# Making the ternary ffn weights inside the context attention instead of beside the projection and the ffn

## The reference

```
x = x + cross_attention(layernorm(x), ctx_2048)      # self attention and context attention, then projection
x = x + sparse_attention(layernorm(x))               # pairwise scores, top 6 keys
def absmean_quant(w):                                # w1: 2048 x 512, w2: 512 x 2048
    scale = mean(abs(w)); return sign(w) * (abs(w) >= 0.7 * scale)
h   = gelu(einsum('bsd,fd->bsf', layernorm(x), absmean_quant(w1)) + b1)
out = x + einsum('bsf,df->bsd', h, absmean_quant(w2)) + b2
```

## Time and profile before

| | |
|---|---|
| median of 3 runs | 2142.95 us (2142.57 to 2144.84) |
| the profiled execution, its own time | 2141.61 us |
| its span, first to last instruction | 2140.3 us |
| busy: PE, DVE, ACT, POOL | 91%, 55%, 44%, 31% |
| moved by DMA | 255.73 MB |
| mean granted TensorE clock | 0.961 |

### The profile page before, as it was taken

One profiled execution on the slowest core, in us unless ns is written; L12 is line 12 of the kernel. 1 busy time (PEld: TensorE's weight loads), 2 busy tenths in 40 slices (PEclk: granted clock), 3 DMA queues, 4 the chain that ended last, 5 costly groups with the idle time before them and its releaser, 6 DMA issues. The chain is left out here.

```text
span 2140.3 us, 30622 instructions
## 1 busy us (share of the span) xinstructions
...
## 2 busy tenths in 40 slices
...
GB/s 197 188 239 178 109 158 118 146 90 130 130 149 84 144 120 111 100 160 134 105 116 122 137 107 135 132 124 84 144 121 115 74 41 274 142 21 3 1 79 20
DMA packets 213130, 255.73 MB, mean 119 GB/s; under 512 B 62120, under 2 KB 132392, under 8 KB 212464
## 3 DMA queue, kind: packets, MB, share of 16 engines
...
q10 hardware_dynamic: 8448, 0.43, 0.2%
q0 software_dynamic: 2048, 0.43, 0.1%
...
## 5 line engine op out<-in xcount | busy, mean ns | idle before, releaser
L480 PE MATMUL kx_ps<-ctxT_hi,wk_hi 128*128 128x400 f32 (+1 forms) x1024 | 366.3, 358 | 15.7 <-DVE ctxT_lo L288 14.4
L482 PE MATMUL kx_ps<-ctxT_lo,wk_hi 128*128 128x400 f32 (+1 forms) x1024 | 356.1, 348 | 0.0
L484 PE MATMUL kx_ps<-ctxT_hi,wk_lo 128*128 128x400 f32 (+1 forms) x1024 | 355.9, 348 | 0.0
L563 PE MATMUL u_ps<-ctxN_hi,pt_hi 128*128 128x512 f32 (+1 forms) x832 | 341.7, 411 | 8.4 <-DVE pt_lo L772 8.4
L564 PE MATMUL u_ps<-ctxN_lo,pt_hi 128*128 128x512 f32 (+1 forms) x832 | 330.5, 397 | 0.0
L565 PE MATMUL u_ps<-ctxN_hi,pt_lo 128*128 128x512 f32 (+1 forms) x832 | 329.2, 396 | 0.0
L772 DVE TENSOR_TENSOR pt_lo<-t_ps,pt_hi 128x512 fp32r<-128x512 f32 (+1 forms) x256 | 144.6, 586 | 277.2 <-ACT pt_hi L987 277.2
L956 ACT ACTIVATE kx_hi<-kx_ps 128x400 fp32r<-128x400 f32 (+1 forms) x256 | 129.2, 505 | 344.9 <-PE kx_ps L484 341.5
L700 DVE TENSOR_TENSOR kx_lo<-kx_ps,kx_hi 128x400 fp32r<-128x400 f32 (+1 forms) x256 | 146.9, 574 | 233.9 <-ACT sq L958 233.5
L987 ACT ACTIVATE pt_hi<-t_ps 128x512 fp32r<-128x512 f32 (+1 forms) x256 | 125.5, 523 | 304.1 <-PE t_ps L548 304.1
L754 DVE CUSTOM_DVE_ANT_0 prob<-sc_ps,rstd_bc 128x400 f32<-128x400 f32 (+2 forms) x256 | 136.4, 570 | 139.1 <-PE sc_ps L536 139.1
...
## 6 DMA issues: line engine op xcount, KB each, us to landing
...
stage<-in_ctx_n SPq DMA_DIRECT2D x96, 256.0 KB, 6.1
wk_hi<-scratch_wk_s SPq DMA_DIRECT2D x56, 256.0 KB, 3.1
wk_lo<-scratch_wk_s SPq DMA_DIRECT2D x56, 256.0 KB, 3.7
wv_hi<-scratch_wv_s SPq DMA_DIRECT2D x56, 256.0 KB, 4.0
wv_lo<-scratch_wv_s SPq DMA_DIRECT2D x56, 256.0 KB, 4.7
scratch_own_rows<-out_sb SPq DMA_DIRECT2D x32, 256.0 KB, 3.1
```

What stands on the lines that cost most here:

```text
L480: PE.matmul(kx_ps[:, j % 2, 0:w], wk_hi[:, g % 2, i, :], ctxT_hi[:, i, c0:c0 + w], start=(i == 0), stop=False)
L482: PE.matmul(kx_ps[:, j % 2, 0:w], wk_hi[:, g % 2, i, :], ctxT_lo[:, i, c0:c0 + w], start=False, stop=False)
L484: mm = PE.matmul(kx_ps[:, j % 2, 0:w], wk_lo[:, g % 2, i, :], ctxT_hi[:, i, c0:c0 + w], start=False, stop=(i == C - 1))
L563: PE.matmul(u_ps[:], pt_hi[0:w, t % 2, cols], ctxN_hi[0:w, y, :], start=(y == 0), stop=False)
```

## The change

Both weights are cut into 32 chunks of 128 x 512 (16 each). In rounds 9 to 24 two chunks a round are loaded into the buffers `wk_raw` and `wv_raw`, unused since round 8, and summed by ScalarE at the end of its round. The totals are taken in round 24 on VectorE; in round 25 TensorE adds them up over the partitions and waits for the two thresholds. In rounds 26 to 41 two chunks a round are loaded again, compared on GpSimd (into one buffer `t_below`), turned into ternary values by VectorE at the end of its round, and one round later stored to scratch memory by SyncE; the next load into a buffer waits until its store has landed. The pair stage loads w1 ready-made, the ffn w2. Class `Ternary` is gone.

```
# attend (G_ = 8)
+        SUMS, MAKES = G_ + 1, G_ + 18
...
+            def ternary_total():                                   # TensorE
+                PE.wait_ge(t_row_total, 1)
+                PE.wait_ge(o_moved, MAKES)
+                for j in range(4):
+                    mm = PE.matmul(t_ps[32 * j:32 * j + 32, 1, 256:258], ones[:], t_total[:], start=True, stop=True)
+                mm.then_inc(t_totalled, 1)
+                PE.wait_ge(t_thr_set, 2)
...
                     keys(n + 3, 2)
+                if n == MAKES - 1:
+                    ternary_total()
                 if s:
                     turn_prob(n + 1, 0)
...
+            def ternary_make(k):                                   # VectorE
+                w = k // 16
+                V.wait_ge(t_lower, k + 1)
+                V.scalar_tensor_tensor(t_raw[k % 2], t_raw[k % 2], t_thr[:, 0, w:w + 1], t_below[:], ALU.is_ge,
+                                       ALU.subtract).then_inc(t_made, 1)
...
                 refill(7)
+                if n == MAKES - 2:
+                    ternary_row_total()
+                if MAKES <= n < MAKES + 16:
+                    ternary_make(2 * (n - MAKES))
+                    ternary_make(2 * (n - MAKES) + 1)
...
+            def ternary_sum(k):                                    # ScalarE, behind refill(7), rounds 9 to 24
+                A.wait_ge(t_in[k % 2], 16 * (k // 2 + 1))
+                A.activation(t_raw[k % 2], t_raw[k % 2], ACTF.Abs,
+                             accum_out=t_sums[:, k // 16, k % 16:k % 16 + 1]).then_inc(t_summed, 1)
...
+            def ternary_below(k):                                  # GpSimd
+                w = k // 16
+                G.wait_ge(t_in[k % 2], 16 * (17 + k // 2))
+                G.wait_ge(t_thr_set, 2)
+                after(G, t_made, k)
+                G.tensor_scalar(t_below[:], t_raw[k % 2], t_thr[:, 1, w:w + 1], None, ALU.is_le).then_inc(t_lower, 1)
...
                     own_norm(u + 1)
+                if MAKES <= n < MAKES + 16:
+                    ternary_below(2 * (n - MAKES))
+                    ternary_below(2 * (n - MAKES) + 1)
...
+            def load_ternary(k, again):                            # SyncE
...
+                else:
+                    SP.wait_ge(t_kept[k % 2], 16 * (k // 2))
+                SP.dma_start(t_raw[k % 2], src).then_inc(t_in[k % 2], 16)
...
                 refill(3, 4)
+                if MAKES < n <= MAKES + 16:
+                    store_ternary(2 * (n - 1 - MAKES))
+                    store_ternary(2 * (n - 1 - MAKES) + 1)
+                for first_n, again in ((SUMS, False), (MAKES, True)):
+                    if first_n <= n < first_n + 16:
+                        load_ternary(2 * (n - first_n), again)
+                        load_ternary(2 * (n - first_n) + 1, again)
# project_out
-                if n == 6:
-                    w1.vector_total()
-            w1.vector_threshold(total_ps[:, 0:1])
-            for i in range(4):
-                after(V, w1.s.done, i)
-                w1.vector_below(i, below[:])
-                w1.vector_quarter(i, below[:], w1.s.below_dve, i + 1)
...
-                if n == 5:
-                    w1.scalar(junk[:])
...
-                if n == 2:
-                    w1.sync(dram["ffn_w1T"])
# sparse_attention, behind the loads of its own weights
+            SP.dma_start(w1[:].bitcast(F32), dram["w_t"][0:16, :, :].rearrange("k p o -> p k o")).then_inc(w1_in, 16)
# ternary_ffn
-            w2.tensor(m_ps[:, 0:1])
-            PE.wait_ge(w1.s.done, 4)
+            PE.wait_ge(w1_in, 16)
...
-            w2.vector_total()
-            w2.vector_threshold(m_ps[:, 0:1])
-            w2.vector_below(0, below[:, 0, :])
-            w2.vector_quarter(0, below[:, 0, :], w2.s.below_dve, 5)
...
-                if f % 4 == 0 and f < 12:
-                    q = f // 4 + 1
-                    w2.vector_quarter(q, below[:, q % 2, :], w2.s.below_pool, q)
...
-            w2.scalar(junk[:])
...
-            for q in range(1, 4):
-                after(G, w2.s.done, 4 + q - 1 if q > 1 else 0)
-                w2.gpsimd_below(q, below[:, q % 2, :])
...
-            w2.sync(dram["ffn_w2T"])
+            for q in range(4):
+                SP.dma_start(w2[:, 4 * q:4 * q + 4, :].bitcast(F32),
+                             dram["w_t"][16 + 4 * q:20 + 4 * q, :, :].rearrange("k p o -> p k o")).then_inc(w2_in[q], 16)
```

More of the change, by code:

```diff
@@ L389, in attend @@
         own_p, own_pT, own_o = sb("own_p", [P, P]), sb("own_pT", [P, 2, P]), sb("own_o", [P, 2, P])
+        t_raw, t_below = [x.wk_raw, wv_raw], sb("t_below", [P, 512], mybir.dt.uint8)
+        t_raw = [buf[:].rearrange("p c d -> p (c d)") for buf in t_raw]
+        t_sums, t_total, t_thr = sb("t_sums", [P, 2, 16]), sb("t_total", [P, 2]), sb("t_thr", [P, 2, 2])
         own_st, own_mv = sb("own_st", [P, 3, 6]), sb("own_mv", [P, 3, 2])
@@ L1100, in scalar @@
                 refill(7)
+                if SUMS <= n < SUMS + 16:
+                    ternary_sum(2 * (n - SUMS))
+                    ternary_sum(2 * (n - SUMS) + 1)
         def gpsimd():
@@ L1280, in store_item, with store_ternary @@
                                  ).then_inc(out_stored[t], 16)
+            def load_ternary(k, again):
+                w, i = divmod(k, 16)
+                if w == 0:
+                    src = dram["ffn_w1T"][P * (i // 4):P * (i // 4) + P, 512 * (i % 4):512 * (i % 4) + 512]
+                else:
+                    src = dram["ffn_w2T"][P * i:P * i + P, :]
+                if not again:
+                    SP.wait_ge((wk_split, wv_split)[k % 2], G_)
+                    after(SP, t_summed, k - 1)
+                elif k < 2:
+                    SP.wait_ge(t_summed, 32)
+                else:
+                    SP.wait_ge(t_kept[k % 2], 16 * (k // 2))
+                SP.dma_start(t_raw[k % 2], src).then_inc(t_in[k % 2], 16)
+            def store_ternary(k):
+                SP.wait_ge(t_made, k + 1)
+                SP.dma_start(dram["w_t"][k, :, :], t_raw[k % 2]).then_inc(t_kept[k % 2], 16)
             x.load_wk(0)
@@ L1361, in sync @@
             for r in range(2):
+                SP.wait_ge(t_kept[r], 16 * 16)
+            for r in range(2):
                 SP.wait_ge(o_stored[r], 16 * (N // 2))
@@ L1447, with project_out @@
-class TernarySignals:
-    def __init__(self, core):
-        self.landed = [core.sem(f"ternary_in{i}") for i in range(4)]
-        self.summed, self.row_totalled, self.totalled = core.sem("t_abs"), core.sem("t_row_total"), core.sem("t_total")
-        self.ones_set, self.thr_set = core.sem("t_ones"), core.sem("t_threshold")
-        self.below_pool, self.below_dve, self.done = core.sem("t_below_pool"), core.sem("t_below_dve"), core.sem("ternary")
-def project_out(core, x2, w1):
+def project_out(core, x2):
@@ L1903, in sparse_attention, with ternary_ffn @@
         sync()
[L1906 removed]
+def ternary_ffn(core, x3, w1, w1_in):
     dram = core.dram
@@ L1916, in ternary_ffn @@
         o_ps = core.ps(stack, "o_ps_e", [P, 4, 512])
-        m_ps = core.ps(stack, "m_ps_e", [P, 512])
-        w2 = Ternary(core, signals, 1, stack, "w2t", [P, 16, 512])
-        w2.place(stack, "e")
-        below, junk = sb("below_e", [P, 2, 2048]), sb("junk_e", [P, 2048])
+        w2 = sb("w2t", [P, 16, 512], F32R)
         xn, xT = sb("xn_e", [P, 4, 512]), sb("xT_e", [P, 4, 512])
@@ L1926, in ternary_ffn @@
         banks = [h_ps[:, 0, :], h_ps[:, 1, :]]
+        w2_in = [sem(f"w2_in{q}") for q in range(4)]
         x_split, hidden_done, gelu_done = sem("x_split"), sem("hidden_done"), sem("gelu_done")
@@ L1935, in hidden @@
                 for c in range(4):
-                    PE.matmul(h_ps[:, f % RING, :], w1.w[:, c, f * P:(f + 1) * P], x_hi[:, c, :], start=(c == 0), stop=False)
-                    mm = PE.matmul(h_ps[:, f % RING, :], w1.w[:, c, f * P:(f + 1) * P], x_lo[:, c, :], start=False,
+                    PE.matmul(h_ps[:, f % RING, :], w1[:, 4 * c + f // 4, f % 4 * P:f % 4 * P + P], x_hi[:, c, :], start=(c == 0), stop=False)
+                    mm = PE.matmul(h_ps[:, f % RING, :], w1[:, 4 * c + f // 4, f % 4 * P:f % 4 * P + P], x_lo[:, c, :], start=False,
                                    stop=(c == 3))
```

99 lines of the change are left out of this document (24 added, 75 removed).

## The result

The changed kernel takes 2172.45 us (median of 4 runs, 2169.52 to 2173.78) against 2143.89 for the kernel before on the same chip: ratio 1.0127, 95% interval 1.0107 to 1.0147. Run once more beside other kernels it took 2168.60 (1.0102, 1.0085 to 1.0119). So it is slower, by 23 to 29 us where 14.7 were forecast.

What follows compares the result with a forecast made beforehand. The prediction took TensorE to bound attend, and chains through VectorE the last stages. Gains of 24.6 against costs of 39.3 gave net +14.7 us, 2156.3 on the profiled execution and 2157.5 as median, range 2142 to 2176.

Steps and rivals of the forecast that it cites:

- Gains, -24.6: Behind attend: removed ternary work gives back 11.4 us in project_out (up to x2) and 13.2 in the ffn.
- the rival that the ffn doesn't give back: ffn: bound by something the waits hide, so 13 us are missing and the time is 2170; chance 0.05.
- The load of w1: Pair stage: w1's 4 MB load is covered by the stage's own work, zero cost; some 16 us if uncovered.
- The chain of an odd round: Attend, six ordinary odd rounds: comparison, make, comparison, make, `pt_lo` in turn start TensorE 3.0 us late; +18.0.
- So I count no fall.: Ordinary odd rounds: the clock stays up behind a 3.0 us wait, judged nearer to 2.63 than 3.58; nothing added.
- The rival: Clock falls behind each 3.0 us wait, six rounds losing 1.9 more (+11), late even-round transfers +7: 2176; chance 0.17.
- Rounds 31 and 39, +12.6: Attend, g = 7: context loads stand behind ternary stores and loads on SyncE; 4.74 wait plus 1.6 clock, as round 7.
- Even rounds, +3.5: Attend, rounds 28 to 40: store, load, comparisons, makes barely fit; 0.3 us a round, 1.0 in rounds 28 and 36.
- Thresholds, +2.2: Attend, round 25: TensorE waits once for VectorE behind its `kx_lo`, 1.7 us plus 0.5 for two tiny operations.
- Sums, +3.0: Attend, rounds 9 to 24: ScalarE's sums fit its waits, except 1.5 us each in rounds 15 and 23.
- the comparison at the cast's rate: Attend, GpSimd: a comparison takes 0.62 us, costs equal gains, 2143.5, no change; chance 0.12.
- Attend hides all: Attend: VectorE's slack before `pt_lo` hides all the added work, so the kernel is faster, 2118; chance 0.07.

Runs made afterwards that it cites:

- gain_alone: Changed kernel without any ternary work in attend; pair stage and ffn load as many bytes of other ready-made halves: 2119.32 us, ratio 0.9876.
- below_first: Changed kernel with GpSimd's two comparisons of a round ahead of `own_norm` instead of behind it: 2157.45 us, ratio 1.0058.
- one_a_round: Changed kernel making one chunk a round in 32 rounds (26 to 57) instead of two in 16: 2144.09 us, ratio 0.9998.
- filled: Changed kernel with 20 matmuls that nobody reads, given to TensorE in its wait for `pt_lo` behind odd rounds with makes: 2164.63 us, ratio 1.0088.
- sums_alone: Changed kernel keeping the sums and their loads, without threshold, comparisons, makes and stores: 2124.16 us, ratio 0.9900.
- best: Changed kernel with comparisons on VectorE, stores early, sums and makes kept out of g = 7 rounds, thresholds one key chunk earlier: 2120.28 us, ratio 0.9882.

## Why the prediction was wrong where it was

The direction and the mechanism held, the time lay inside the range, and the forecast size was half of the measured one.

- *Gains, -24.6.* Right in sum: 25.2 in the trace, 23.4 in gain_alone; the rival that the ffn doesn't give back is out. The parts are off by more: up to x2 10.1 came back where 11.4 were forecast, from x2 to the end 15.2 where 13.2 were, beyond the outer end of 14. The load of w1 cost nothing, as forecast: from x2 to the ffn's first transpose it is 168.6 us before and 168.8 now.
- *The chain of an odd round, "TensorE starts 3.0 late".* Right: TensorE is idle 2.96 to 2.97 in all six and starts 3.2 late, with each link near its price; below_first and one_a_round show that `own_norm` ahead and the second comparison make it. Rounds with the wait and no fall take 27.77 against 24.57 in round 35, the same 3.2, and so do those of filled, where TensorE is hardly idle.
- *"So I count no fall."* **This step failed.** The sum put the clock's fall at nothing in the six ordinary odd rounds. It costs 1.5 (29.3 against 27.77 in rounds 35 and 41 of two executions; once 2.6, round 29 of the second), and came in four of the six rounds both times: +6.2 in the first trace, out of the 10.0 by which the ternary work in attend cost more than forecast. filled shows that it is the clock: with TensorE kept busy the same delay costs 3.2. The argument from the idle times 2.63 and 3.58 took the length of the wait for what decides. The rival had the mechanism and overstated it, 1.9 in each of six; that its 2176 lies so near is partly luck, since the 7 us that it adds for late transfers in even rounds came to 0.8.
- *Rounds 31 and 39, +12.6.* Right in kind, 14.6 in size; the waits were 6.3 and 5.2 instead of 4.7. The 4.7 was taken over from round 7, where SyncE's stop was given as the cause. Here that is only one of two: with the stores early the rounds stay at 32.6 and 32.4, with the comparisons on VectorE at 33.2 and 33.6, and only both edits bring them to 26.4 and 27.1. That the size came out near is partly luck.
- *Even rounds, +3.5.* Taken together right (4.3), but all of it stood in 28, 30 and 36 (1.8, 0.8, 1.7) and none in the others. In 28 and 36 pieces of the context stand between the makes and `pt_lo`, as foreseen; they cost 1.8 and 1.7 where 1.0 was given.
- *Thresholds, +2.2*: 2.0. *Sums, +3.0*: 3.9 in the first trace, 4.6 by sums_alone; right rounds, and the fall of the clock in round 23 is the part that was missed.
- *Rival: the comparison at the cast's rate.* Ruled out by L1216 at 1.56 and more. *Attend hides all*: not in this form; it does in best.

In one account of the first trace: 39.3 forecast, 6.2 for the clock, 2.0 for g = 7, 0.8 for even rounds, 0.9 for sums, 0.7 for the 0.2 more of delay in four rounds less the 0.2 of the thresholds, less the 0.6 by which rounds 29 and 37 came out below 3.0, is 49.3; the 57.4 measured hold 7.6 of scatter besides, and 0.5 is open. By medians the work in attend costs 2172.45 or 2168.60 less 2119.32, so 53 or 49. What remains open is what decides whether the clock falls behind a wait of 2 to 3 us.
